# Eight token norms of a transformer tower: seven of them made tile by tile, with the reciprocal root taken by GpSimd

## The reference

```python
h = _L0_tok_ref(x, ...)
h = _layernorm(h + _L0_attn_ref(h, ...), axis=-1)
h = _layernorm(h + _L0_ffn_ref(h, ...), axis=-1)
h = _layernorm(h + _L1_attn_ref(h, ...), axis=-1)
h = _layernorm(h + _L1_ffn_ref(h, ...), axis=-1)
h = _layernorm(h + _L2_attn_ref(h, ...), axis=-1)
h = _layernorm(h + _L2_ffn_ref(h, ...), axis=-1)
h = _layernorm(h + _L3_attn_ref(h, ...), axis=-1)
h = _layernorm(h + _L3_ffn_ref(h, ...), axis=-1)
```

## Time and profile before

| | |
|---|---|
| median of 3 runs | 1320.39 us (1316.8 to 1324.31) |
| profiled execution, its own time | 1309.12 us |
| span of its instructions | 1307.5 us |
| busy: PE, DVE, ACT, POOL | 903.5, 636.0, 427.5, 215.1 us |
| granted TensorE clock, mean | 0.815 of full speed |

### The profile page before, as it was taken

One profiled execution on the slowest core, in us unless ns is written; L12 is line 12 of the kernel. 1 busy time (PEld: TensorE's weight loads), 2 busy tenths in 40 slices (PEclk: granted clock), 3 DMA queues, 4 the chain that ended last, 5 costly groups with the idle time before them and its releaser, 6 DMA issues. The chain is left out here.

```text
span 1307.5 us, 25828 instructions
## 1 busy us (share of the span) xinstructions
PE 903.5 (69%) x9931; PEld 739.1 (57%) x9931; DVE 636.0 (49%) x1464; ACT 427.5 (33%) x728; POOL 215.1 (16%) x240
## 2 busy tenths in 40 slices
PE   4936666654656469828988557857677999476684
PEld 1335555522333359726878556646447999464573
DVE  1637777636776343166444233645463111256354
ACT  0148888512333112123334322334220111133132
POOL 2122222110000134213112001010012332100100
PEclk9969999976665579968888758968586999879598
DMA  4323333276000358010000060000052996100000
GB/s 120 83 87 113 115 114 114 79 191 145 1 0 1 98 174 204 19 49 2 2 2 2 1 156 9 4 1 3 1 133 68 225 256 144 32 2 3 1 4 20
DMA packets 63923, 90.67 MB, mean 69 GB/s; under 512 B 16532, under 2 KB 51016, under 8 KB 63824
## 3 DMA queue, kind: packets, MB, share of 16 engines
q1 hardware_dynamic: 58320, 83.57, 23.4%
q0 software_dynamic: 5504, 5.70, 2.2%
HBM read 81.66 MB, written 8.12 MB: 69 GB/s over the span
## 5 line engine op out<-in xcount | busy, mean ns | idle before, releaser
L1752 PE MATMUL ps_rows<-stage_strip,stage_hat_y 128*128 128x144 f32 x800 | 110.4, 294 | 73.1 <-ACT stage_hat_y L1719 73.1
L1752 PEld LDWEIGHTS ps_rows<-stage_strip,stage_hat_y 128*128 128x128 f32 x800 | 102.1, 193 | 81.4 <-ACT stage_hat_y L1719 50.1
L1783 DVE TENSOR_TENSOR stage_product<-ps_rows,stage_hat_x 128x1296 f32<-128x1296 f32 x80 | 68.9, 902 | 42.8 <-PE ps_rows L1752 42.8
L2559 DVE TENSOR_TENSOR L_ffnhid<-L_ffnact_gate,L_ffnbank_u 128x300 f32<-128x300 f32 x32 | 15.0, 467 | 117.6 <-ACT L_ffnact_gate L2577 117.6
L1791 DVE TENSOR_REDUCE stage_samples<-stage_product 128x1440 f32 x40 | 66.2, 1655 | 9.3 <-DVE stage_product L1783 9.3
L1714 ACT ACTIVATE stage_hat_y<-stage_hat_y,stage_w_minus_row 80x1280 f32<-80x1280 f32 x40 | 54.5, 1362 | 45.8 <-DMA stage_hat_y<-places_y 45.8
L1734 POOL TENSOR_TENSOR stage_hat_x<-stage_pos_xT,stage_w_window_x 128x240 f32<-128x240 f32 x80 | 48.4, 627 | 125.0 <-DVE stage_product L1783 118.9
L1556 PE MATMUL ps_conv<-stage_w_offset_w,stage_patches 128*100 128x512 f32 x96 | 44.8, 620 | 17.6 <-DMA stage_patches<-in_patchesT 17.6
L1719 ACT ACTIVATE stage_hat_y<-stage_hat_y 80x1280 f32<-80x1280 f32 x40 | 50.1, 1253 | 0.0
L1135 PE MATMUL L_attnbank_q<-L_attnhT,L_attnwq 97*128 97x200 f32 x192 | 43.6, 374 | 6.9 <-DVE L_attnqT L1298 6.7
L1135 PEld LDWEIGHTS L_attnbank_q<-L_attnhT,L_attnwq 97*128 97x128 f32 x192 | 36.8, 213 | 9.4 <-issue 8.7
(11 more groups left out here) (430 smaller groups left out, 2176.3 us busy)
## 6 DMA issues: line engine op xcount, KB each, us to landing
stage_hat_y<-places_y SPq DMA_DIRECT2D x40, 400.0 KB
L_ffn_win<-in_L_ffn_Win SPq DMA_DIRECT2D x10, 1152.0 KB, 8.9
stage_L_ffn_win<-in_L_ffn_Win SPq DMA_DIRECT2D x6, 1152.0 KB, 9.2
L_ffnranks<-stage_ranks SPq DMA_DIRECT2D x16, 400.0 KB
L_ffn_win<-in_L_ffn_Win SPq DMA_DIRECT2D x8, 768.0 KB, 14.0
L_ffn_wout<-in_L_ffn_Wout SPq DMA_DIRECT2D x10, 576.0 KB, 6.3
stage_L_ffn_wout<-in_L_ffn_Wout SPq DMA_DIRECT2D x6, 576.0 KB, 6.5
stage_strip<-in_strips SPq DMA_DIRECT2D x160, 19.7 KB
```

The costliest lines, as they stand in the source:

```text
L1752: mm = nc.tensor.matmul(ps[:, p % 2, bank, at * cols:(at + 1) * cols], hat_y[:, p, g, h * P:(h + 1) * P], rhs.rearrange("q j c x -> q (j c ...
L1783: last = nc.vector.tensor_tensor(split(product[:, p % 2, slots.start * cols:slots.stop * cols]), ps[:, p % 2, banks, 0:used * cols].rearra ...
```

## The change

`tw.mean` is no tensor of its own any more but the first column of `mean_var`, so nothing copies it. A new class `TokenNorm` makes the norm in the main block of stages 2 to 8: behind each tile's `bn_stats` VectorE makes this tile's `bn_aggr` and adds eps into `rstd` (each step waits for the one before), and GpSimd, at the end of its queue in that block, waits for all eight tiles and raises `rstd` to the power -0.5 in one instruction on 128 x 8. The block `finish_norm` is gone from these seven stages, and stays in stage 1, without its copy. In stages 2 and 6 the final loop goes by pairs of tiles, step by step for both.

```diff
-        self.mean = self.sb("mean", [P, TILES, 1])
+        self.mean = self.mean_var[:, :, 0:1]
...
             dve.wait_ge(aggregated, TILES)
-            nc.vector.tensor_copy(tw.mean[:], tw.mean_var[:, :, 0:1])
             dve.wait_ge(rooted, 1)
...
+class TokenNorm:
...
+    def stats(self, t):
+        self.nc.vector.bn_stats(self.tw.moments[:, t, :], self.tw.y[:, t, :]).then_inc(self.measured, 1)
+
+    def aggregate(self, dve, t):
+        dve.wait_ge(self.measured, t + 1)
+        self.nc.vector.bn_aggr(self.tw.mean_var[:, t, :], self.tw.moments[:, t, :]).then_inc(self.aggregated, 1)
+
+    def add_eps(self, dve, t):
+        dve.wait_ge(self.aggregated, t + 1)
+        self.nc.vector.tensor_scalar(self.tw.rstd[:, t, :], self.tw.mean_var[:, t, 1:2], LN_EPS, None, ALU.add).then_inc(self.var_ready, 1)
+
+    def invert(self, pool):
+        rstd = self.tw.rstd[:].rearrange("p t o -> p (t o)")
+        pool.wait_ge(self.var_ready, TILES)
+        self.nc.gpsimd.tensor_tensor(rstd, rstd, self.tw.minus_half[:].to_broadcast([P, TILES]), ALU.pow).then_inc(self.rstd_ready, 1)
+        pool.wait_ge(self.rstd_ready, 1)
...
                 dve.wait_ge(y_ready, t + 1)
-                nc.vector.bn_stats(tw.moments[:, t, :], tw.y[:, t, :])
+                token_norm.stats(t)
+                token_norm.aggregate(dve, t)
+                token_norm.add_eps(dve, t)
...
                 for f in range(PAIRS):
                     store_keys(f)
+            token_norm.invert(pool)
...
-            for t in range(TILES):
-                dve.wait_ge(y_loaded[t // 2], 16)
-                nc.vector.bn_stats(tw.moments[:, t, :], tw.y[:, t, :])
+            for c in range(4):
+                two = (2 * c, 2 * c + 1)
+                dve.wait_ge(y_loaded[c], 16)
+                for t in two:
+                    token_norm.stats(t)
+                for t in two:
+                    token_norm.aggregate(dve, t)
+                for t in two:
+                    token_norm.add_eps(dve, t)
...
             attention(tw, "L2_attn", "unit", w5)
-            finish_norm(tw, "L2_attn")
```

More of the change, by code:

```diff
@@ L2345, in _ @@
                     list_rows(e + AHEAD)
-            for t in range(TILES):
-                dve.wait_ge(y_loaded[t // 2], 32)
-                nc.vector.scalar_tensor_tensor(out=tw.y[:, t, :], in0=back[:, t, :], scalar=m.total[:, t, :], in1=m.h[:, t, :], op0=ALU.mult, op1=ALU.add).then_inc(s["first_added"], 1)
-                dve.wait_ge(s["first_added"], t + 1)
-                nc.vector.scalar_tensor_tensor(out=tw.y[:, t, :], in0=back[:, TILES + t, :], scalar=m.first[:, t, :], in1=tw.y[:, t, :], op0=ALU.mult, op1=ALU.add).then_inc(s["added"], 1)
-                dve.wait_ge(s["added"], t + 1)
-                nc.vector.bn_stats(tw.moments[:, t, :], tw.y[:, t, :])
+            for c in range(4):
+                two = (2 * c, 2 * c + 1)
+                dve.wait_ge(y_loaded[c], 32)
+                for t in two:
+                    nc.vector.scalar_tensor_tensor(out=tw.y[:, t, :], in0=back[:, t, :], scalar=m.total[:, t, :], in1=m.h[:, t, :], op0=ALU.mult, op1=ALU.add).then_inc(s["first_added"], 1)
+                for t in two:
+                    dve.wait_ge(s["first_added"], t + 1)
+                    nc.vector.scalar_tensor_tensor(out=tw.y[:, t, :], in0=back[:, TILES + t, :], scalar=m.first[:, t, :], in1=tw.y[:, t, :], op0=ALU.mult, op1=ALU.add).then_inc(s["added"], 1)
+                for t in two:
+                    dve.wait_ge(s["added"], t + 1)
+                    token_norm.stats(t)
+                for t in two:
+                    token_norm.aggregate(dve, t)
+                for t in two:
+                    token_norm.add_eps(dve, t)
         @block.scalar
@@ L2837, in stage_3 @@
             branch_attention(tw, "L1_attn", w3)
-            finish_norm(tw, "L1_attn")
         plan[3] = stage_3
```

25 lines of the change are left out of this document (15 added, 10 removed).

## The result

The changed kernel takes 1322.50 us (median of 20 runs, 1318.45 to 1340.33) against 1317.09 of the kernel before on the same chip (20 runs, 1306.93 to 1335.79). The ratio is 1.0049, with a 95% interval of 1.0026 to 1.0071: some 6 us slower, where 1.0 was forecast. The profiled execution took 1319.88 us on a span of 1318.2, its mean granted clock was 0.804.

What follows compares the result with a forecast made beforehand. No engine is full; the seams between stages lie wholly on the path. Terms -0.4 - 0.5 + 2.4 - 1.0 + 0.45 = +1.0 us on 1320.4 give 1321.4 us, range 1313 to 1329.

Steps and rivals of the forecast that it cites:

- The power, 1.59 us: At each of seven stage ends, GpSimd's power on 128 x 8 takes 0.23 fixed plus 1.36 us.
- The bounds 0.37 and 2.27: Ends for the power's us: the smaller multiplication (total takes 8.5), or cost independent of element number (total adds 4.8).
- rival 1: Faster: the power costs like a multiplication, 0.25 us for eight elements; seams win 9.4 more, 1312. Chance 0.06.
- Rival 2: Faster: a table load costs more than its row, ScalarE being flushed around it; 10.2 us more won, 1311. Chance 0.03.
- Five seams: From last `bn_stats` to next norm; all seven forecast at 24.2 us against 24.6, -0.4 us.
- The way out: Engine meetings and semaphore clearing behind the reciprocal at seven stage ends: 9.61 us, taken as unchanged with GpSimd arriving last.
- if the way out is not near 1.37 a stage: Stated sign that the prediction is wrong: the time for leaving a stage departs from about 1.37 us.
- The loops, +2.4: Attention loops: VectorE's added norm steps delay later work; 0.4 in stages 4 and 8 each, 0.8 in 5, 0.8 to 0.9 in 7.
- Table load in the router, -0.5: Stage 8's router: the exponential no longer waits for its own table load, -0.5 us.
- Stage 2's final loop, -1.0: Going by pairs, the last addition ends 8.85 us from the start, against 9.43 + 0.40: -1.0 us.
- Stage 6, +0.45: Second half of stage 6: each pair takes 0.95 us with norm steps, so the last addition ends 0.45 us later.
- Rival 3: Slower: VectorE bounds the attention loops, steps passing in full on 24 shifts, 9.6 us instead of 2.4; 1328.6. Chance 0.07.

Runs made afterwards that it cites:

- early_drain: The changed kernel with a drain of GpSimd's queue ahead of the wait for the variances in stages 2 and 6; ratio to the kernel before 1.0058, repeated 1.0065.
- old_norm_2_6: The changed kernel with the norm of stages 2 and 6 taken back to the old block of its own; ratio to the kernel before 1.0040.
- split_power: The changed kernel with each power cut in parts (tiles 1 to 6 early, 7 and 8 alone, together in stages 2 and 6); ratio to the kernel before 1.0019.
- drain_norms_first: The changed kernel with GpSimd's queue drained early in stages 2 and 6 and memsets behind the first two norms in 3, 5, 7; ratio to the kernel before 0.9974.

## Why the prediction came into its range, and what in it was wrong

The time, 1322.50 us, came into the range (1313 to 1329) and 1.1 us from the forecast of 1321.4. That closeness is luck: the median of three runs on which it was built, 1320.39, stands 3.3 us above the 1317.09 of twenty, and this covers most of the error. Forecast was a change of +1.0 us, and measured is +6.5 (3.4 to 9.3). By its steps:

- **The power, 1.59 us: right.** 1.647 is the mean of seven instances. The bounds 0.37 and 2.27 are gone, and rival 1 with them; by the cycles an element that the Trainium skill, GPSIMD Engine Reference, section "Elementwise — side-by-side cycle accounting", gives, its estimate was 0.25, and the measurement decides. Rival 2, a table load dearer than its row, is gone too: the five seams without an indirect transfer would each be over a microsecond shorter than they are.
- **Five seams: right** but for one. Each is within 0.04 us of the kernel before. Against the prediction's own sum stages 3, 5, 7 and 8 are within 0.04 and stage 4 is 0.36 over (3.70 against 3.34), in its way out.
- **The way out, "9.61 us for seven, I leave": wrong.** This is the step that failed. I had seen that GpSimd arrives last in place of VectorE and costed only its wait for its own result. The block's end also drains its queue, and behind indirect transfers this takes 2.7 us; before, it was over 11 us (stage 2) and 4 us (stage 6) ahead of VectorE's last `bn_stats`. Stages 2 and 6 are longer by 2.67 and 2.26 us, **+4.9**, and `early_drain` takes 5.0 out of the seams. No rival had this case; the only slower ones were VectorE as the bound and a dear power. The text named the sign of being wrong ("if the way out is not near 1.37 a stage"), and there it was.
- **What follows a seam: not asked.** The prediction has no term for the next stage's start. It gave **-2.3 us** (starts 11.24 to 8.91), all by the order of two instructions 0.3 us apart.
- **The loops, +2.4: right.** Stage 7 +0.87 (forecast 0.8 to 0.9); stages 4 and 8 +0.22 each (forecast 0.4). Behind `bn_stats` the next step began 0.69 us after its start, where 0.66 was forecast. Stage 5 +1.0 (forecast 0.8), at the same clock of 0.70. Together 2.3.
- **Table load in the router, -0.5: right.** From the last step ahead of it to the exponential the load is gone, and the next step stands 0.46 us earlier.
- **Stage 2's final loop, -1.0**: from its start to the last addition's end 9.08 us, forecast 8.85, so the term was too large by a quarter. **Stage 6, +0.45**: from the start of the fifth `bn_stats` to the end of the eighth it took 1.55 us with the norm steps, against 1.14, so the term is right. The stage from first norm to last `bn_stats` is 1.0 us longer all the same, and 0.7 of it lie ahead of the first `bn_stats`. `old_norm_2_6`, without norm steps in that stage, has this too (197.34 before, 198.29 there), so it is not their cost; its cause stays open.
- **Rival 3, VectorE as the bound of the loops: no.** It needed 8 us in the loops, and 2.3 were there.

The remainder is the clock. Over the 88 compared runs the kernel before had a mean granted clock of 0.8064, the changed one over 18 runs 0.8029, which is 0.0034 less (0.0014 either way). Within the runs of the kernel before, 0.01 of clock goes with 6.6 us; that makes 2.3 us. (A small part of this is counted twice: the seams and starts that changed stand at a granted clock of 0.50, so 2.6 us more of them lower the mean of 1318 us by themselves, by an estimated 0.0006.) With -2.3 from the starts, +4.9 from the seams, +2.3 from the loops, -0.8 in stage 2, +1.0 in stage 6 and -0.5 in the router the sum is near 7, and without the clock's share near 4.6; both are in the interval. Whether the change caused the lower clock, or whether any shift of the work would have, no run here tells. For eleven altered sets the clock of the kernel before in the same comparison is on record. Nine of them are lower; `split_power` (0.8060 against 0.8052) and `drain_norms_first` (0.8073 against 0.8070) are not. The unaltered kernel run again is lower too, within its error.

## What to carry to other kernels

Whoever puts an engine's instruction last before engines meet must cost all that the engine still does behind it: drain a queue that has issued indirect transfers early, under a wait, and keep it off the meeting. Look at what starts on the far side as well: a GpSimd memset that begins ahead of VectorE's first norms held them here for its whole length, and one wait that puts it behind them won it back. And where identical kernels differ by 5 us in one stage, read an edit's cost from seams and from stretches with the same clock in both traces, and run several edits together and apart before believing in a median.

## What the runs showed that I had not expected

- A drain of GpSimd's queue ends 2.8 us behind the last indirect transfer's row when it is issued at once (stage 2; 3.5 us in stage 6), and still takes 2.68 us when 16 us have passed since that row (552.6 to 568.4). Behind the power of stage 3, which has no such transfers, it takes 0.034, and after an early drain 0.047. So the waiting did not pay it off, and a drain did.
- A `tensor_scalar` of 0.38 us lasts 1.02 to 4.52 us beside memsets of GpSimd, always to about 0.1 us behind the end of one.
- The clock of TensorE took different courses in executions of one and the same kernel (0.91 and 0.50 in the same 20 us of stage 3) behind stretches that read nearly alike: TensorE busy 10.49 and 10.62 us in the 20 us before, at a clock of 0.76 both.
- A GpSimd power costs 0.157 us for each element of a partition on 0.39 fixed, in one to twelve elements.
